# A graph attention layer: key/value rows made once and gathered, groups of 16 nodes split in two halves, scored and summed in four 32-row column tiles

## The chip, the cores and the metric

The kernel runs on one core of one Trainium2 chip. The metric is the device time of the whole program in microseconds (us), a median of several runs. A profile is one execution taken by the hardware profiler. TensorE (PE) multiplies matrices and transposes; VectorE (DVE), ScalarE (ACT) and GpSimd (POOL) work on elements; SyncE (SP) and POOL issue the DMAs here.

## The reference, cut to what matters

`x` is 6250 x 256; there are 206250 edges with 64 attributes each, sorted by destination, 33 to a node on average. Eight heads of 32 columns. The part that the change touches:

```python
x0 = layernorm(x)
q = (x0 @ Wq.T + bq); k = (x0 @ Wk.T + bk); v = (x0 @ Wv.T + bv)   # each (n, 8, 32)
e = (edge_attr @ We.T).reshape(-1, 8, 32)
alpha = sum(q[dst] * (k[src] + e), axis=-1) / sqrt(32)             # per edge and head
ex = exp(alpha - amax[dst])
out = segment_sum((v[src] + e) * ex / denom[dst])                  # per node and head
```

A gated skip, two layer norms, a feed-forward net of 1024 and a small mixture of experts follow; they are the third stage.

## The kernel before

All is fp32. N is padded to 6272 nodes, NB = 49 blocks of 128; a block has GB = 8 groups of GN = 16 nodes. Each group has one window of CH = 640 edges (T = 5 tiles of 128) from the place where its edges begin; edges of other nodes in the window are masked by a comparison of `dst` with the node number (`neq`, L530).

**Stage 1** (L122 to L297) normalizes x into `xn_rows` in HBM, makes `qT` (queries, transposed, kept in SBUF) and finds where each group's edges begin (`offs`). It goes in seven chunks of seven row tiles.

**Stage 2** (L302 to L792) is a loop over blocks and, written out in it, over the eight groups (turn j). Weights are folded into the queries and out of the values: for each group `G` = q times Wk (per head) is made on TensorE (`g_piece`, L680), so that scores are `G` times normalized rows, and values are summed as rows of x and edge attributes (`pZ`, 128 rows = 16 nodes x 8 heads, 321 columns) and projected with WvT only once a block (L783 to L791). In turn j:

- SyncE waits for `slot_free` (L444) and issues the loads for group j+2: `dst` broadcast (L403), `edge_attrT` (L405), `edge_attr` (L406), then the indices `srci` for group j+3 (L397). Once a block `starts` (L410) reads offsets into registers.
- POOL waits for the same count and for the indices, and issues five indirect DMAs (`gather`, L490), each of 128 rows of `xn_rows`, for group j+2.
- TensorE: `scores` of group j+1 (L694: six matmuls of 320 columns into `pS`); then five `pZ` matmuls of group j (L763), whose last frees the slot, with the transposes of the gathered rows of group j+2 (`ft`, L688) and the pieces of `G` between them; then `pt` (L703, five transposes of the weights of group j+1) and `zt` (L737, three transposes of group j's sums).
- DVE: `neq`, the maximum over `pS` (L536), the copies `pt_out` (L542) and `zt_out` (L586); once a block the merge into `U` (L606, L608), for which TensorE's next `zt` waits.
- ACT: copies of the transposed rows `FT` and of `G` (L622), `Exp` of the scores (`weights`, L636), `Zs` (L666).

There are four slots `F` and `F3`, so loads run two groups ahead. The order on each engine is the written one. The loop around all blocks (`long_loop`, L387) runs again only if some group has more edges than CH.

**Stage 3** (from L794) is node-wise and reads `U` and `xn_rows`.

Of the kernel before, what the change touches and what calls it, by code (L numbers as in the profile page):

```python
# [45 lines left out]
def build(nc, a, out):  # L46
# [16 lines left out]
    FW = 3 * P  # L63
    ONE = D + DE
    FP = -(-(ONE + 1) // 4) * 4
    K3 = DE + 1 + GN
    ZW = D + DE + 1
# [9 lines left out]
    BC = -(-(NG + 1) // P)  # L77

    xn_d = nc.dram_tensor("xn_rows", [NP, D], F32, kind="Internal").ap()
    bound_d = nc.dram_tensor("bounds", [BC * P], I32, kind="Internal").ap()  # L80
    x_d = a["x"].rearrange("(b p) d -> p b d", p=P)
    xn_v = xn_d.rearrange("(b p) d -> p b d", p=P)
    dst_rows = a["dst"].rearrange("(r c) -> r c", c=P)
# [3 lines left out]
    def sem(name):  # L87
        return top.enter_context(nc.semaphore(name))
# [12 lines left out]
    with top:  # L101
# [10 lines left out]
        offs = sbt(top, "offs", [1, NG + GB], I32)  # L112
# [3 lines left out]

        mid = ExitStack()
        with mid:
            qT = sbt(mid, "qT", [P, KD, NP + P])
            with ExitStack() as s1:  # L120
                x_all = sbt(s1, "x_all", [P, NB, D])
                xs = sbt(s1, "xs", [P, W7, D])  # L122
                xT = sbt(s1, "xT", [P, KD, W7 * P])
# [6 lines left out]
                WqT = sbt(s1, "WqT", [P, KD, D])  # L130
                bq = sbt(s1, "bq", [P, KD])
# [12 lines left out]
                lens = sbt(s1, "lens", [1, NG])  # L144
                mlen = sbt(s1, "mlen", [1, 1])
                tp = [pst(s1, f"tp{i}", [P, KD, P]) for i in range(2)]
                pq = [pst(s1, f"pq{i}", [P, 4 * P]) for i in range(2)]

                x_landed, w_landed, first_landed = sem("x_landed"), sem("w_landed"), sem("first_landed")
                rows_gathered, bounds_stored, bounds_landed = sem("rows_g"), sem("bounds_stored"), sem("bounds_landed")  # L150
                tiles_seen, xs_free = sem("tiles_seen"), sem("xs_free")
                U_cleared = sem("U_cleared")
                store_turns1 = sem("store_turns1")
                stats_done, rstd_done, xn_ready, xn_stored = sem("stats_done"), sem("rstd_done"), sem("xn_ready"), sem("xn_st")
                tp_filled, tp_emptied, q_filled, q_emptied = sem("tp_f"), sem("tp_e"), sem("q_f"), sem("q_e")
                bval_ready, rowi_ready, start_ready = sem("bval_r"), sem("rowi_r"), sem("start_r")
                q_steps = [(h0, min(4, W7 - h0)) for h0 in range(0, W7, 4)]
                Q7 = len(q_steps) * KD

                with nc.Block() as block:  # L160
# [112 lines left out]
                    def _(pe):  # L273
# [3 lines left out]
                        with pe.Fori(0, N7) as i:  # L277

                            pe.wait_ge(q_emptied, i * Q7 + 1)
                            for j in range(W7):  # L280
                                pe.wait_ge(xn_ready, i * W7 + j + 1)
                                if j >= 2:
                                    pe.wait_ge(tp_emptied, i * W7 + j - 1)
# [1037 lines left out]
```

## Time and profile before

| | us |
|---|---|
| median of 3 runs | 5581.74 |
| lowest, highest | 5575.02, 5582.84 |
| span of the profiled execution | 5584.0 |
| TensorE busy (share) | 5115.2 (92%) |
| ACT busy | 2257.3 (40%) |
| DVE busy | 1934.3 (35%) |
| POOL busy | 1895.7 (34%) |

Busy time is that of an engine's own instructions; DMA issues on SyncE do not count as busy, and each has a duration of its own in the time line (SPq). TensorE's entries are matmuls (PE) and weight loads (PEld); their ends are modelled, so distances between starts are the safer measure. Idle time of an engine names what ended it in square brackets. "PEclk" is the granted TensorE clock as a share of 2.4 GHz.

### The profile page before, as it was taken

The numbers are of one execution on the slowest core, as the hardware profiler recorded it, in microseconds if no ns is written. First come the engines' busy times: TensorE is split into PE (matmuls) and PEld (weight loads), VectorE is DVE, ScalarE is ACT, GpSimd is POOL, SyncE is SP. The second block draws the span as 40 slices with busy tenths as digits, with TensorE's granted clock in tenths as the row PEclk, the third lists the DMA queues.
The fourth block names the chain that finished last, engine by engine and source line by source line (L and its number), as shares of the span: only waits on it lengthen the run. The fifth ranks groups of instructions, "written<-read, shape, count | busy, mean of one in ns | idle before, by whom it ended". The sixth has DMA issues, their size and how long they took to land. (4 is left out here: it accounts for less than half of the span.)

```text
span 5584.0 us, 76757 instructions
## 1 busy us (share of the span) xinstructions
PE 5115.2 (92%) x22479; PEld 3611.0 (65%) x22479; DVE 1934.3 (35%) x4447; ACT 2257.3 (40%) x4140; POOL 1895.7 (34%) x2013
## 2 busy tenths in 40 slices
PE   4899999999999999999999999999999677877778
PEld 2577777777777777777777677777776454544545
DVE  3233233233333333333333332322333445445454
ACT  2344444444444444444444444444444323233233
POOL 1444444444444444444444444444443000000000
PEclk9899999999999999999999999999999877788778
DMA  2333333333333333333333433433433100000000
GB/s 102 94 103 96 96 100 98 97 98 94 102 96 96 103 95 95 102 92 95 103 95 95 105 94 92 104 93 96 103 94 86 61 13 20 13 13 20 13 13 7
DMA packets 486457, 445.39 MB, mean 80 GB/s; under 512 B 359613, under 2 KB 389310, under 8 KB 486408
## 3 DMA queue, kind: packets, MB, share of 16 engines
q0 software_dynamic: 96384, 265.00, 17.4%
q1 hardware_dynamic: 390024, 179.92, 12.8%
q14 instruction: 41, 0.34, 0.0%
q8 instruction: 8, 0.13, 0.0%
HBM read 431.89 MB, written 12.82 MB: 80 GB/s over the span
## 5 line engine op out<-in xcount | busy, mean ns | idle before, releaser
L494 POOL DMA_INDIRECT F<-xn_rows,srci x1970 | 1865.8, 947 | 2283.6 <-PE pZ L763 1799.4
L622 ACT ACTIVATE FT<-ring 128x256 f32<-128x256 f32 x1970 | 1196.9, 653 | 2328.9 <-PE ring L691 2327.2
L763 PE MATMUL pZ<-F,PT 128*128 128x321 f32 x3920 | 1380.7, 434 | 0.0
L699 PE MATMUL pS<-FT,G 128*128 128x320 f32 x3144 | 1096.0, 474 | 78.0 <-ACT FT L622 77.6
L699 PEld LDWEIGHTS pS<-FT,G 128*128 128x128 f32 x3144 | 613.0, 205 | 371.4 <-issue 202.2
L546 DVE COPY PT<-pPT 128x384 f32<-128x384 f32 (+1 forms) x786 | 348.8, 485 | 1327.8 <-PE pPT L706 1327.8
L691 PEld LDWEIGHTS ring<-ident,F 128*128 128x128 f32 x3940 | 481.5, 141 | 493.8 <-ACT FT L622 221.9
L691 PE MATMUL ring<-ident,F 128*128 128x128 f32 x3940 | 775.7, 282 | 7.4 <-DMA F<-xn_rows,srci 6.3
L763 PEld LDWEIGHTS pZ<-F,PT 128*128 128x128 f32 x3920 | 668.5, 191 | 105.0 <-issue 1.6
L539 DVE TENSOR_REDUCE nmx<-pS 128x1 f32<-128x640 f32 x393 | 324.0, 824 | 940.0 <-PE pS L699 935.3
L699 PE MATMUL pS<-F,G 81*128 81x320 f32 x1572 | 585.0, 454 | 0.0
L639 ACT ACTIVATE Pw<-pS,nMn 128x640 f32<-128x640 f32 x393 | 531.1, 1351 | 7.1 <-DVE nMn L540 7.1
L699 PEld LDWEIGHTS pS<-F,G 81*128 81x128 f32 x1572 | 319.4, 203 | 141.9 <-issue 28.2
L787 PE MATMUL pM<-WvT,ZT 128*128 128x33 f32 (+1 forms) x2352 | 365.7, 326 | 5.1
L787 PEld LDWEIGHTS pM<-WvT,ZT 128*128 128x128 f32 (+1 forms) x2352 | 359.1, 246 | 16.8 <-DVE ZT L589 16.8
L928 POOL DMA_DIRECT2D out_dram<-accb x6 | 5.8, 959 | 1072.5 <-DVEq L1093 1072.5
L706 PE MATMUL pPT<-ident,Pw 128*128 128x128 f32 x1965 | 279.4, 273 | 2.5 <-ACT Pw L639 2.5
L589 DVE COPY ZT<-pM 128x384 f32<-128x384 f32 x392 | 214.9, 548 | 192.2 <-PE pM L744 192.2
L622 ACT ACTIVATE G<-ring 128x256 f32<-128x256 f32 (+1 forms) x595 | 252.6, 425 | 13.4 <-PE ring L685 13.3
L685 PE MATMUL ring<-qh,Wk 128*128 128x256 f32 x794 | 237.9, 382 | 11.2 <-DVE qh L552 11.2
L1204 PE MATMUL hid<-rT,W1T 128*128 128x512 f32 (+1 forms) x448 | 204.1, 616 | 35.5 <-ACT h L1136 27.8
L533 DVE TENSOR_SCALAR F<-F,nid 17x640 f32<-17x640 int32 x394 | 214.6, 545 | 56.1 <-DVE U L608 44.0
(180 smaller groups left out, 3975.2 us busy)
## 6 DMA issues: line engine op xcount, KB each, us to landing
F<-in_edge_attrT SPq DMA_DIRECT2D x394, 160.0 KB
F<-in_edge_attr SPq DMA_DIRECT2D x394, 160.0 KB, 3.8
F<-xn_rows,srci POOLq DMA_INDIRECT x1970, 2.8
F<-in_dst SPq DMA_DIRECT2D x394, 42.5 KB
srci<-in_src SPq DMA_DIRECT2D x395, 2.5 KB, 3.3
x_all<-in_x SPq DMA_DIRECT2D x1, 6272.0 KB, 22.1
xn_rows<-xs SPq DMA_DIRECT2D x7, 896.0 KB, 3.9
xnb<-xn_rows SPq DMA_DIRECT2D x7, 896.0 KB, 4.8
```

The costliest lines, as they stand in the source:

```text
L494: pool.indirect_dma_start(out=F[s][:, t, 0:D], out_offset=None, in_=xn_d, in_offset=bass.IndirectOffsetOnAxis(ap=srci[j % GB][:, t:t + 1], ...
L539: ch.step(dve.tensor_reduce(nmx[:, j:j + 1], pS[:, :, 0:SH], AX.XY, ALU.max, negate=True))
L546: dve.tensor_copy(PT[:, t0:t1, :], pPT[q][:, 0:(t1 - t0) * P].rearrange("p (t r) -> p t r", r=P)).then_inc(pt_emptied, 1)
L589: dve.tensor_copy(ZT[:, :, :, j * GN:(j + 1) * GN], pM[:, 0:FW].rearrange("p (k h n) -> p k h n", k=3, n=GN)).then_inc(zt_emptied, 1)
L622: act.activation(dst, src, ACT.Copy).then_inc(ring_emptied, 1)
L639: act.activation(Pw[:, :, :].rearrange("p t (a e) -> p a e t", a=2), pS[:, :, 0:SH].rearrange("p a (e t) -> p a e t", t=T), ACT.Exp, bias= ...
L685: pe.matmul(ring[n % 2][0:rows, 0:HR * P // 2], w, qh[half][:, c, :, :].rearrange("p r n -> p (r n)"), start=True, stop=True).then_inc(rin ...
L691: m = pe.transpose(ring[n % 2][:, k * P:(k + 1) * P], F[j][:, t, k * P:(k + 1) * P], ident[:, :])
L699: m = pe.matmul(pS[:, q, 0:SH], G[0:(P if k < KD else K3), k, j, :], f, start=(k == 0), stop=(k == 2))
L706: m = pe.transpose(pPT[q][:, (t - t0) * P:(t - t0 + 1) * P], Pw[:, t, :], ident[:, :])
L763: z = pe.matmul(pZ[:, 0:ZW], PT[:, t, :], F[s][:, t, 0:ZW], start=(t == 0), stop=(t == T - 1))
L787: pe.matmul(pM[:, h * CW:(h + 1) * CW], ZT[0:rows, k, h, :], WvT[0:rows, k, h, :], start=(k == 0), stop=(k == 2))
```

## The change

Stage 1 additionally projects every row tile with [Wk, Wv] into `kv_rows` (512 columns: keys and values in blocks of 64, biases added by DVE) in HBM, and writes the scaled queries to `q_cols` in HBM instead of SBUF. x lands in seven pieces in `U`, whose clearing POOL does chunk by chunk; the masks are built here.

Stage 2 keeps 392 groups of 16 nodes, but a group consists of two halves of ON = 8 nodes with windows of OW = 320 edges each; `offs` has an entry for each half. The gather takes 512 columns of `kv_rows` in place of 256 of `xn_rows`, still five indirect DMAs of 128 rows. Scores: rows of `pS` are four strips of 32 (two sets of four heads x two halves), each written by its own matmul of 320 columns, twice (queries times keys; `G3` times edge attributes and mask). `pS` is 384 columns wide (320 + 64 of overlap of the halves). The sums `pZ` are 3 x 4 matmuls of 192 columns, each into 32 rows. `Pw` has three transposes, `Zs` two. The per-block projection becomes `project`, run in turn 0 of the next block, and the merge in its turn 1. SyncE loads each half by itself and fetches 64 queries twice a block.

```diff
+    ON = GN // 2
+    NO = 2 * NG
+    OW = CH // 2
+    HP = P // 2
+    SW = OW + HP
+    KB = SW // P
+    KV = 2 * D
+    FP = KV + DE
+    ZW = P + DE
...
+                            for j in range(W7):
+                                project_rows(i, j)
+                                if i + 1 < N7:
+                                    transpose_rows(i + 1, j)
...
-                            sp.dma_start(srci[j % GB][:, :], a["src"][bass.ds(o, CH)].rearrange("(p t) -> p t", t=T)
-                                         ).then_inc(idx_landed[j % GB], 16)
+                            s, done = srci[j % GB], idx_landed[j % GB]
+                            sp.dma_start(s[:, 0:TO], a["src"][bass.ds(oa, TO * P)].rearrange("(t p) -> p t", p=P)).then_inc(done, 16)
+                            sp.dma_start(s[0:HP, TO:TO + 1], src_t[bass.ds(oa, HP)].rearrange("(p t) -> p t", t=1)).then_inc(done, 16)
+                            sp.dma_start(s[HP:P, TO:TO + 1], a["src"][bass.ds(ob, HP)].rearrange("(p t) -> p t", t=1)).then_inc(done, 16)
+                            sp.dma_start(s[:, TO + 1:T], src_b[bass.ds(ob, TO * P)].rearrange("(t p) -> p t", p=P)).then_inc(done, 16)
...
+                            for o, at in enumerate((oa, ob)):
+                                cols = slice(o * OW, (o + 1) * OW)
+                                sp.dma_start(F3[s][DE:K3, cols].bitcast(I32), dst_t[bass.ds(at, OW)].partition_broadcast(GN)
+                                             ).then_inc(f3_landed[s], 16)
+                                sp.dma_start(F3[s][0:DE, cols], a["edge_attrT"][:, bass.ds(at, OW)]).then_inc(f3_landed[s], 16)
+                            sp.dma_start(F[s][:, 0:TO, KV:FP], a["edge_attr"][bass.ds(oa, TO * P), :].rearrange("(t p) d -> p t d", p=P)
                                          ).then_inc(ea_landed[s], 16)
+                            sp.dma_start(F[s][0:HP, TO, KV:FP], ea_t[bass.ds(oa, HP), :]).then_inc(ea_landed[s], 16)
+                            sp.dma_start(F[s][HP:P, TO, KV:FP], a["edge_attr"][bass.ds(ob, HP), :]).then_inc(ea_landed[s], 16)
+                            sp.dma_start(F[s][:, TO + 1:T, KV:FP], ea_b[bass.ds(ob, TO * P), :].rearrange("(t p) d -> p t d", p=P)
+                                         ).then_inc(ea_landed[s], 16)
...
                         def scores(j, s):
 
+                            half, g = j // HB, (j % HB) * 2
+                            for x in range(2):
+                                for c in range(KD):
+                                    for o in range(2):
+                                        r = c * HP + o * C
+                                        rows, cols = slice(r, r + C), slice(o * HP, o * HP + OW)
+                                        if x == 0:
+                                            m = pe.matmul(pS[rows, cols], qh[half][:, c, g + o, :],
+                                                          FT[j % 2][:, c, o * OW:(o + 1) * OW], start=True, stop=False)
+                                        else:
+                                            m = pe.matmul(pS[rows, cols], G3[half][0:K3, c, g + o, :],
+                                                          F3[s][0:K3, o * OW:(o + 1) * OW], start=False, stop=True)
                             m.then_inc(s_done, 1)
...
+                        def z_part(s, t):
+
+                            for c in range(KD):
+                                for o in range(2):
+                                    rows = slice(c * HP + o * C, c * HP + (o + 1) * C)
+                                    blocks = F[s][:, o * TO + t, :].rearrange("p (x d) -> p x d", d=BLK)
+                                    f = blocks[:, 2:9:3, :] if c == 0 else blocks[:, 6:9, :]
+                                    m = pe.matmul(pZ[rows, 0:ZW].rearrange("p (x d) -> p x d", d=BLK), PT[:, t, rows], f,
+                                                  start=(t == 0), stop=(t == KB - 1))
+                            return m
...
+                            for c in range(KD):
+                                pe.matmul(byhead[:, c * HR:(c + 1) * HR, 0:C], outT[:, c, :, :].rearrange("p a n -> p (a n)"),
+                                          ident[:, :].rearrange("p (h c) -> p h c", c=C), start=(c == 0), stop=False)
+                            for h in range(HR):
+                                pe.matmul(pairs[:, :, h, 0:C], zeaT[:, h, :, :].rearrange("p a n -> p (a n)"), WeP[:, h, :].rearrange("p (k c) -> p k c", k=KD),
+                                          start=False, stop=False)
...
                                     for t in range(KB):
                                         z = z_part(s, t)
                                         if t == KB - 1:
                                             z.then_inc(slot_free, 1)
                                         if t == 0:
                                             pe.wait_ge(gathered[s2], it * (16 * T * 2) + 16 * T * ((j + 2) // SLOTS + 1))
                                         pe.wait_ge(ring_emptied, rb + (m + t - 1))
                                         ft(s2, t, RING0 + m + t)
```

## Rows read from the trace of the kernel before

**Rows 1.** The page's part 1: busy us, share of the span, instructions.
```profile
PE 5115.2 (92%) x22479; PEld 3611.0 (65%) x22479; DVE 1934.3 (35%) x4447; ACT 2257.3 (40%) x4140; POOL 1895.7 (34%) x2013
```

**Rows 2.** Line 606, the merge: duration min/median/max ns, first and last start us.
```profile
L606 DVE TENSOR_TENSOR Utmp<-U,pM x49: 428/429/430, 268.1 to 4322.3; 128x264 f32<-128x264 f32 x49
```

**Rows 3.** Windows: stretch and its length, each engine's busy us, clock, DMA.
```profile
core 0: us, PE busy (x) PEld busy (x) DVE busy (x) ACT busy (x) POOL busy (x), PEclk, DMA share, GB/s
2000.00:2084.40 84.40, 82.73 (x393) 60.01 (x392) 26.00 (x58) 36.40 (x70) 37.88 (x40) 0.94 0.38 98
...
2039.30:2045.10 5.80, 5.80 (x13) 3.76 (x14) 1.40 (x3) 0.00 (x0) 0.00 (x0) 0.52 0.00 0
...
6.00:20.00 14.00, 0.00 (x0) 0.00 (x0) 7.66 (x10) 0.00 (x0) 4.03 (x4) 1.00 1.09 387
```

**Rows 4.** Time line of TensorE over one turn: start us, us, what, xcount.
```profile
2002.54 0.71 PE L706 MATMUL pPT<-ident,Pw 128*128 128x128 f32 x5
2003.09 0.49 PE L744 MATMUL pM<-ident,Zs 128*128 128x128 f32 x3
2003.80 1.31 PE L699 MATMUL pS<-FT,G 128*128 128x320 f32 x4 [0.23 <-ACT FT L622]
...
2007.12 0.70 PE L763 MATMUL pZ<-F,PT 128*128 128x321 f32 x2
2007.66 0.38 PE L691 MATMUL ring<-ident,F 128*128 128x128 f32 x2
...
2011.55 0.71 PE L706 MATMUL pPT<-ident,Pw 128*128 128x128 f32 x5
```

**Rows 5.** Time line of TensorE, the projection at a block's end.
```profile
2031.44 7.61 PE L787 MATMUL pM<-WvT,ZT 128*128 128x33 f32 x48
```

**Rows 6.** Waits of SyncE's queue: us in total, times, longest.
```profile
SPq L444 <- PE pZ L763: 3016.6, 390, 28.9
```

**Rows 7.** Time line of SyncE's queue: index load, then a group's loads.
```profile
147.88 0.47 SPq L397 DMA_DIRECT2D srci<-in_src  x1
148.47 0.26 SPq L403 DMA_DIRECT2D F<-in_dst  x1
148.83 0.49 SPq L405 DMA_DIRECT2D F<-in_edge_attrT  x1
149.51 0.59 SPq L406 DMA_DIRECT2D F<-in_edge_attr  x1
150.29 0.49 SPq L397 DMA_DIRECT2D srci<-in_src  x1
```

**Rows 8.** Line 411, reads of offsets into registers: duration min/median/max ns.
```profile
L411 SPq TENSOR_LOAD <-offs x50: 892/2052/2097, 144.3 to 4212.1; - x50
```

**Rows 9.** The page's part 6: DMA issues, KB each, us to landing.
```profile
F<-xn_rows,srci POOLq DMA_INDIRECT x1970, 2.8
...
srci<-in_src SPq DMA_DIRECT2D x395, 2.5 KB, 3.3
```

**Rows 10.** Time line of POOL: a gather of 512 B rows, two of 1 KB.
```profile
15.66 0.96 POOL L191 DMA_INDIRECT drow<-in_dst,rowi  x1 [0.30 <-issue]
...
2003.05 0.95 POOL L494 DMA_INDIRECT F<-xn_rows,srci  x1 [3.69 <-PE pZ L763]
...
2004.30 0.95 POOL L494 DMA_INDIRECT F<-xn_rows,srci  x1 [0.30 <-issue]
```

**Rows 11.** DMA queues from 2000 to 2084 us: packets, MB, share of engines.
```profile
q0 software_dynamic: 1886, 5.17, 22.8%
q1 hardware_dynamic: 7184, 2.99, 15.2%
```

**Rows 12.** Time line of TensorE in stage 1: projections of two chunks.
```profile
84.78 6.18 PE L294 MATMUL pq<-xT,WqT 128*128 128x512 f32 x16
...
94.98 6.18 PE L294 MATMUL pq<-xT,WqT 128*128 128x512 f32 x16
```

More of the change, by code:

```diff
@@ L233, in _ @@
[L233 to L245 removed]
+                        dve.wait_ge(bias_landed, 16 * (3 + KD))
@@ new lines, in project_rows @@
+                        def project_rows(i, j):
+                            n = i * W7 + j
+                            if n >= 3:
+                                pe.wait_ge(kv_emptied, n - 2)
+                            for f in range(KD):
+                                m = pe.matmul(pkv[n % 3][:, :], xT[i % 2][:, f, j * P:(j + 1) * P], Wkv[:, f, :],
+                                              start=(f == 0), stop=(f == KD - 1))
+                            m.then_inc(kv_filled, 1)
+                        for j in range(W7):
+                            transpose_rows(0, j)
@@ L410, in starts, with load_q @@
+                        def load_q(half, first):
+                            sp.dma_start(qb[half][:, :, :], q_v[:, :, bass.ds(first, HP)]).then_inc(qb_landed[half], 16)
                         def starts(first, n):
@@ L649, in _ @@
                         for j in range(2):
-                            for t in range(T):
-                                ft_out(j, t, n, n + 1)
+                            for q in range(len(PAIRS)):
+                                ft_out(j, q, n, n + 1)
                                 n += 1
                         weights(0, 1)
-                        with long_loop(act) as e0:
-                            ps = e0 // CH
+                        longest, loop = long_loop(act)
+                        with loop as e0:
+                            ps = e0 // OW
@@ L688, in ft, with g3 @@
-                        def ft(j, t, n):
-                            for k in range(KD):
-                                m = pe.transpose(ring[n % 2][:, k * P:(k + 1) * P], F[j][:, t, k * P:(k + 1) * P], ident[:, :])
+                        def g3(half):
+                            for c in range(KD):
+                                m = pe.matmul(pM[0:DE, c * HR * HP:(c + 1) * HR * HP], We[:, c, :],
+                                              qh[half][:, c, :, :].rearrange("p x r -> p (x r)"), start=True, stop=True)
+                            m.then_inc(g3_filled, 1)
```

759 lines of the change are left out of this document (423 added, 336 removed).

## The prediction

> **What bounds the kernel now.** I read the page's busy shares first: TensorE is busy 92% of the span, no other engine over 40% [rows 1]. A share over the span hides stages, so next the turns. The merge at L606 runs 49 times, the first at 268.1 us, the last at 4322.3 us [rows 2]: 4054.2 / 48 = 84.5 us for a block of 128 nodes, 10.56 us for one of its eight groups, and 49 x 84.47 = 4139 us for the middle stage. Ahead of it lie 268.1 - 84.5 = 184 us, behind it the remaining 1261 us; the change leaves the third stage alone, so all is decided in the middle. The windows say the same: one block of 84.4 us has TensorE 82.7 us busy and POOL 37.9, ACT 36.4, DVE 26.0 [rows 3].
>
> The time line of TensorE shows what a turn is made of [rows 4]. From one `pPT` burst (2002.54) to the next (2011.55) is 9.01 us. Six score matmuls of 320 columns take 2003.80 to 2007.12, 0.553 us each. A `pZ` matmul of 321 columns has its follower 0.54 us later (2007.12 to 7.66), so one of 256 columns counts 0.43; five transposes of `Pw` take 0.55 (2002.54 to 3.09), 0.11 each. Each fp32 matmul is two MATMUL records (x2), a transpose one. Eight turns of 9.01 make 72.1 us, but a block takes 84.5: the missing 12 us are the projection, 24 small matmuls in 7.6 us (0.32 us each) [rows 5], and the scores behind it, 5.8 us for what else takes 3.3, at a granted clock of 0.52, the 1.2 GHz level, where the block's mean is 0.94 [rows 3]. Before that fall TensorE had run short matmuls and weight loads.
>
> Last the queues, off the path today, since SyncE and POOL both wait for `pZ` [rows 6, 10]. A group's four loads are issued start to start 0.59 (indices, 147.88 to 148.47), 0.36 (dst), 0.68 (attrT) and 0.78 us (attr) [rows 7]: 2.4 us. Once a block SyncE reads nine offsets into registers: 2.05 us, and for three of them 0.89 [rows 8]. POOL issues five gathers, 1.25 us apart (2003.05 to 4.30): 6.25 us [rows 10].
>
> **The change, part by part.** *Does the new width fit?* The windows shrink from 640 to 320 edges for 8 nodes, and the loop repeats everything if one half has more. I counted dst of the reference's drawn inputs (seed 0): the longest run of an aligned eight nodes is 308. One pass, as before.
>
> *TensorE in a turn.* Columns after the change, if four 32-row column tiles truly run side by side: scores 2 x 0.553 = 1.11; `pZ` 3 x 192 columns, 3 x 0.54 x 192/321 = 0.97; ten transposes of keys 1.10; three of `Pw` 0.33; two of `Zs` 0.22; `g3` four matmuls of 256 columns a block, 4 x 0.43/8 = 0.21; `project` eight matmuls a block at the projection's 0.32, 0.32. Sum 4.26 us against 10.56. If the tiles run one after another: 8 x 0.553 + 12 x 0.323 + the same 2.18 = 10.48 us. The trace has no 32-row tile, so these are the two ends; the side-by-side end is no cheaper than the streamed columns. I take it, because the tiles of a group of four write different rows of PSUM and nothing in the program makes one wait for another; both ends stay in the range. At the lower clock of [rows 3] (5.8 us for 3.3) the 4.26 would become up to 8.5. The Trainium skill, "TensorEngine Tiling (Array Packing)", Key Properties, says that different tiles can load weights and multiply in parallel, but also that changing the tiling mode drains the engine; the first gives the 4.26, the second would add to it six times a turn, since full-array transposes stand between the tiled parts, and at rival C's price for a stop make it 5.2 to 5.9. No row here shows either.
>
> *SyncE.* This is what I expect to bind. Each load of a group is cut at the half boundary: dst 2, attrT 2, attr 4, indices 4, twelve DMAs for four. By the rows the time of an issue hangs little on size: 0.49 us for 64 rows of 2560 B, 0.59 for 640 pieces of 256 B, 0.47 to 0.49 for 128 rows of 20 B [rows 7]; only dst is at 0.26. So I take start to start 2 x 0.38 + 2 x 0.68 + 4 x 0.72 + 4 x 0.57 = 7.3 us, the attr halves a little under the whole. Low end, the short ones at attrT's 0.68 and the indices at 0.55: 7.0; high end, dst like attrT and all others like attr: 0.68 x 4 + 0.78 x 8 = 9.0. Added: two `load_q` a block, 2 x 0.75/8 = 0.19, and two register reads of ten values; from 0.89 for three and 2.05 for nine, 0.19 a value, so 2.25 each, 0.56 a turn. With a wait, 8.1 us (7.5 to 9.8). Queued behind each wait for `slot_free` are all twelve; who waits for them: DVE's `neq` (dst), TensorE's `pZ` (attr), and POOL, whose gather needs the indices that SyncE issues last. On the skill's page "DMA: Bandwidth & Descriptors", Rules for kernel authors, two transfers to disjoint partition halves are called not worth it, as both use the same 16 DMA engines; by it the halves gain nothing on the bus and cost their issue, which is the direction of this sum.
>
> *POOL.* Five gathers still, with rows of 2 KB for 1 KB. 128 rows of 512 B took 0.96 us and 128 of 1 KB 0.95 [rows 10], so I take 1.25 start to start, 6.25 and some 0.2 of waits: 6.5 us. Hidden while SyncE needs 8.1; its bound if SyncE is cheaper.
>
> *DMA engines.* In a block q0 is 22.8% and q1 15.2% of 84 us [rows 11]: 2.39 and 1.60 us a turn. The gathers double to 1.31 MB: 4.8 us at today's share for each byte, 3.4 at the 387 GB/s of the early `x_all` load [rows 3]. q1 has 7184/8 = 898 packets a turn now [rows 11] and about 1500 after (640 indices of 4 B one by one): 1.6 to 2.7 us. Together 5.0 to 7.5 us of a turn. At 8.1 they are 62 to 93% busy, so landings lengthen.
>
> *Does the chain fit?* Index DMA issued, lands 3.3 us later; five gathers 6.25; the last lands 2.8 us on, more under load [rows 9]; then transposes and `pZ` 1.5: about 14.5 us, within which SyncE has two more turns, 16.2. It fits with little slack. What makes SyncE's turn start is `slot_free`, three turns apart.
>
> *ACT and DVE.* They are 36.4/8 = 4.55 and 26.0/8 = 3.25 us busy a turn now [rows 3], and the change takes columns from both: `Exp`, the maximum and `PT` go from 640 columns to 384, the 1280 key columns go out in three copies for five, the `G` pieces and the `ZT` copies go; added are `halves_out`, six copies of at most 256 columns twice a block, and `g3_out`. So both stay under 4.6 us and hidden behind 8.1. Were the 8.1 gone, the chain scores, maximum, Exp, transposes would be next, at some 5 us.
>
> *Stage 1.* TensorE takes 10.2 us for seven row tiles now (84.78 to 94.98), 6.18 of it for 3584 projected columns, 1.72 ns a column [rows 12]. The key/value rows add 14 matmuls of 512 columns, 12.4 us: 7 x 20.1 = 141 us for 74. That is +67; with x landing in pieces and its statistics ahead of the bounds the loop should start some 24 us sooner (the two waits on DMA round trips leave its path), and the last store adds 6: +49 us (20 to 90; the added stores are 19 MB). DVE's and ACT's work of a chunk, each under half of TensorE's 20 us by [rows 3]'s shares, lies beside it. POOL's mask constants move here, beside that work. Prologue of the middle stage: gathers dominate as now, 0.
>
> *Sum*, against the profiled 5584 us: 5584 - 4139 + 392 x 8.1 + 49 = 4669 us. The runs' median 5581.74 is within 0.05% of the span, so I keep the number: 4670.
>
> **The rivals.** (A) *SyncE is cheaper than its rows, POOL or the DMA engines bind.* For: half-size loads have fewer descriptors, dst shows 0.26. Against: 20-byte rows cost as much as 2560-byte ones. 6.3 to 7.4 us a turn, at 6.9: 5584 - 4139 + 2705 + 49 = 4200. (B) *TensorE stays the bound*, because tiles overlap only in part or the clock falls to the level of [rows 3]. For: TensorE would be half idle, and its clock fell once already. Against: a turn at the low clock is 8.5, only just over SyncE. 9 to 10.2 us, at 9.6: 5260. (C) *Slower: tiles in series, and a stop at each change between tiled and full array.* Place: the six changes in a turn between scores or `pZ` and the transposes. Price: 10.48 plus six times 0.16 to 0.27 (two `pZ` records span 0.70 us where their follower starts after 0.54 [rows 4]; one half is 0.27), 11.4 to 12.1; at 11.7: 5584 - 4139 + 4586 + 49 = 6080. It decides from 10.44 us a turn on (4139 - 49 over 392). For: the columns in series are already 10.48. It is here that the drain of the skill's "TensorEngine Tiling (Array Packing)" page would act. Against: nothing in the program orders the tiles. (D) *A second pass*, if some half exceeded 320: twice the loop, near 7800. The count speaks against it.
>
> **How the numbers follow.** Forecast (SyncE, 7.5 to 8.8 us: 4430 to 4940) 0.50; A (4000 to 4430) 0.22; B (5000 to 5500) 0.18; C 0.08; D and others slower 0.02. Slower than before 0.09, within 0.2% (about what a measurement of this kernel can tell from no change) 0.01, faster 0.90. The predicted time is the likeliest case's 4670; the range leaves out C, D, the top of B and the lowest part of A: 4100 to 5350.
>
> **What would show it.** Right: the L606 successor spaced about 65 us a block; SyncE's DMA starts without gaps over 1 us; TensorE idle before the transposes on a gather or before `pZ`, busy share under 70%; four MATMUL records of a `pZ` quartet starting within 0.4 us. A: POOL gathers without gaps at 1.25 us. B: TensorE over 90% busy with PEclk low. C: quartets spaced as the sum of four. Wrong altogether: SyncE's short DMAs at 0.3 us, or gathers of 2 KB rows longer than 0.95 us to issue.

## The result, and the profile after

The changed kernel takes 5456.15 us (median of 4 runs, 5444.12 to 5460.82) against 5580.15 of the kernel before in the same measurement: ratio 0.9773, 95% interval 0.9759 to 0.9787. It is 2.3% faster, 786 us above the forecast of 4670 and 106 us above the top of the stated range, 5350. The page of its profiled execution, beside [rows 1] and [rows 11]:

```profile
span 5459.2 us, 88133 instructions
...
PE 4078.0 (75%) x26117; PEld 2169.5 (40%) x26117; DVE 1766.1 (32%) x4373; ACT 1362.9 (25%) x3251; POOL 1925.3 (35%) x2075
...
PEclk9777777777777777777777777777777887788778
DMA  5566666666666666666666666666665000000000
...
q0 software_dynamic: 159520, 523.41, 32.3%
q1 hardware_dynamic: 715732, 205.36, 17.7%
```

TensorE lost a fifth of its busy time, from 92% of the span to 75%, and nothing else became full. The merge is at L689 now; its instructions, beside [rows 2] (durations in ns, then first and last start in us):

```profile
L689 DVE TENSOR_TENSOR Utmp<-U,pM x50: 428/429/431, 239.6 to 4198.2; 128x264 f32<-128x264 f32 x50
```

The 49 spacings take 3958.6 us, 80.8 us each, 10.10 us a turn. The first merge of the new order stands in turn 1 of block 0 (it has nothing to add yet) and the last behind the loop, so the 49 spacings hold 391 turns and not 392: a turn is really 10.12. Turns below are all spacings divided by eight; for the changed kernel and what is made from it they are thus some 0.3% low, which no comparison rests on.

Because the merge moved, the stages are better parted at the first and last `pZ` matmul (before, then after):

```profile
L763 PE MATMUL pZ<-F,PT x3920: 431/433/436, 188.8 to 4312.3; 128*128 128x321 f32 x196
```

```profile
L850 PE MATMUL pZ<-F,PT x9408: 322/350/530, 224.0 to 4189.4; 128*32 128x192 f32 x196
```

What lies ahead of the first grew by 35 us, the middle stage fell from 4123.5 to 3965.4 us, by 158, and what lies behind it changed by 2 (1271.7 and 1269.8 us).

The waits say who is late: first those of the compute engines, then SyncE's own for `slot_free`, which were 3016.6 us before [rows 6] (total us, times, longest):

```profile
ACT FT L758 <- remote: 2059.4, 286, 9.6
POOL F L604 <- DMA srci<-in_src: 1467.2, 349, 46.2
...
DVE nmx L656 <- remote: 561.1, 148, 5.6
...
PEld pZ L850 <- issue: 452.7, 1457, 1.5
```

```profile
SPq L587 <- PE pZ L850: 144.0, 86, 4.7
...
SPq L587 <- remote: 86.5, 108, 1.7
```

SyncE hardly waits any longer: it is the queue that binds, and POOL waits for the indices that SyncE issues last. But one kind is new, "remote" on ScalarE and VectorE, and TensorE's weight loads for `pZ` wait 452.7 us for nothing that the profile shows. SyncE's time line shows the same from the other side, beside [rows 7]:

```profile
2005.10 0.44 SPq L545 DMA_DIRECT2D F<-in_edge_attr  x1
2006.17 0.69 SPq L547 DMA_DIRECT2D F<-in_edge_attr  x1
2008.34 0.01 SPq L548 DMA_DIRECT2D F<-in_edge_attr  x1
2009.77 0.00 SPq L549 DMA_DIRECT2D F<-in_edge_attr  x1
2010.48 0.68 SPq L532 DMA_DIRECT2D srci<-in_src  x1
2011.21 0.49 SPq L533 DMA_DIRECT2D srci<-in_src  x1
2011.87 0.47 SPq L534 DMA_DIRECT2D srci<-in_src  x1
```

From 2011.21 on an issue follows the last one after 0.66 us; between 2005.10 and 2010.48 four steps take 5.4 us. I call this a slow stretch. In one, every instruction of SyncE, also one that moves no data, takes some 0.7 us or a multiple, and the streams of other engines crawl too: in this one TensorE's `pZ` records start 0.7 us apart, one by one (2009.82, 2010.52), and ScalarE's copy at 2011.38 has 7.26 us of "remote" before it. POOL is the exception: its gathers go on at 1.25 us start to start (2003.89 to 2008.89). The clearest mark is the register MOVE in front of each DMA (min/median/max in ns). Kernel before, then after:

```profile
L406 SPq MOVE F<-in_edge_attr x394: 29/29/37, 147.0 to 4295.3; - x197
```

```profile
L548 SPq MOVE F<-in_edge_attr x394: 2/29/866, 206.0 to 4176.7; - x197
```

This stretch begins 2.3 us after POOL starts a round of five gathers (2003.89) and ends 2.3 us after the last is issued (2008.89). Nearly every turn has one; others begin up to 6 us into the round and are shorter.

The tiles themselves did what was hoped. TensorE's time line, beside [rows 4]; the first three lines at the granted clock 0.50, the last three at 1.00:

```profile
2028.89 1.30 PE L831 MATMUL pS<-FT,qh 128*32 128x320 f32 x8
2029.96 1.29 PE L834 MATMUL pS<-F,G 80*32 80x320 f32 x8
2031.03 0.87 PE L850 MATMUL pZ<-F,PT 128*32 128x192 f32 x8
...
2036.30 0.75 PE L831 MATMUL pS<-FT,qh 128*32 128x320 f32 x8
2036.87 0.72 PE L834 MATMUL pS<-F,G 80*32 80x320 f32 x8
2037.41 0.51 PE L850 MATMUL pZ<-F,PT 128*32 128x192 f32 x8
```

Four matmuls of 320 columns (x8: two records each) take 0.57 and 0.54 us (2036.30 to 2036.87 to 2037.41), the time of one before the change.

### The profile page after: what moved, and what is told of

It reads as the page before. It is cut to its first block and busy times, and to the rows that moved or that the text cites. A ratio compares the mean times of both kernels' runs of the same rounds, so it can differ in the third digit from the quotient of the medians.

```text
span 5459.2 us, 88133 instructions
## 1 busy us (share of the span) xinstructions
PE 4078.0 (75%) x26117; PEld 2169.5 (40%) x26117; DVE 1766.1 (32%) x4373; ACT 1362.9 (25%) x3251; POOL 1925.3 (35%) x2075
## 5 line engine op out<-in xcount | busy, mean ns | idle before, releaser
L604 POOL DMA_INDIRECT F<-kv_rows,srci x1970 | 1880.9, 955 | 2147.4 <-DMA srci<-in_src 1467.2
L758 ACT ACTIVATE FT<-ring 128x512 f32<-128x512 f32 (+1 forms) x1182 | 581.8, 527 | 2990.7 <-remote 2059.4
L850 PE MATMUL pZ<-F,PT 128*32 128x192 f32 x9408 | 810.0, 390 | 93.5 <-issue 92.0
L662 DVE COPY PT<-pPT 128x384 f32<-128x384 f32 x393 | 219.0, 557 | 1600.1 <-PE pPT L840 1197.3
L656 DVE TENSOR_REDUCE nmx<-pS 128x1 f32<-128x384 f32 x393 | 219.0, 557 | 1027.8 <-remote 561.1
L850 PEld LDWEIGHTS pZ<-F,PT 128*32 128x32 f32 x9408 | 284.7, 125 | 493.8 <-issue 452.7
L831 PE MATMUL pS<-FT,qh 128*32 128x320 f32 x3144 | 436.6, 641 | 14.2 <-issue 12.1
L834 PE MATMUL pS<-F,G 80*32 80x320 f32 x3144 | 415.7, 612 | 0.0
L650 DVE TENSOR_SCALAR F<-F,nid 16x640 f32<-16x640 int32 x394 | 223.0, 566 | 58.3 <-issue 31.8
L764 ACT ACTIVATE Pw<-pS,nMn 128x384 f32<-128x384 f32 x393 | 226.3, 576 | 9.1 <-DVE nMn L657 4.3
```

Of the source, the lines that this page charges most:

```text
L604: pool.indirect_dma_start(out=F[s][:, t, 0:KV], out_offset=None, in_=kv_d, in_offset=bass.IndirectOffsetOnAxis(ap=srci[j % GB][:, t:t + 1] ...
L650: dve.tensor_scalar(F3[j][DE:K3, :], F3[j][DE:K3, :].bitcast(I32), nid[DE:K3, c], None, ALU.not_equal).then_inc(neq_done, 1)
L656: ch.step(dve.tensor_reduce(nmx[:, j:j + 1], pS[:, 0:SW], AX.X, ALU.max, negate=True))
L758: act.activation(FT[j % 2][:, :, t0 * P:t1 * P], ring[n % 2][:, 0:KD * w].rearrange("p (k e) -> p k e", e=w), ACT.Copy).then_inc(ring_empt ...
L764: act.activation(Pw[:, :], pS[:, 0:SW], ACT.Exp, bias=nMn[:, j:j + 1], accum_out=lsum[:, j:j + 1]).then_inc(p_done, 1)
L831: m = pe.matmul(pS[rows, cols], qh[half][:, c, g + o, :], FT[j % 2][:, c, o * OW:(o + 1) * OW], start=True, stop=False)
```

## The experiments

The kernels were measured in five batches; the kernels of a batch ran one after another on one chip, with the kernel before beside them (5606.65, 5582.11, 5583.03, 5577.74 and 5599.76 us in batches 1 to 5). Batches 2 and 3 had the same chip. Some edits gather or load other edges than the layer needs, to time a part by itself; where that is so it is said. Times are medians; a turn is the spacing of the merges divided by eight.

**Batch 1: what are the slow stretches made of?**

*Gathered bytes halved.* 1 KB rows of `xn_rows` are gathered; the value columns are zeros.

```diff
-                                    out=F[s][:, t, 0:KV], out_offset=None, in_=kv_d,
+                                    out=F[s][:, t, 0:D], out_offset=None, in_=xn_d,
```

> The gather takes 256 columns of xn_rows again in place of 512 of kv_rows (1 KB rows for 2 KB; the value columns stay zero, so the sums are not the reference's); all else is the changed kernel. Theory T: SyncE's queue sets the turn, 12 issues of about 0.65 us, and a stretch of 2 to 3 us in each turn in which all engines' instructions come only every 0.7 us, which comes with the DMA engines at a share near 1, so with the gathered bytes. T expects no such stretch, a turn of 8.0 to 8.5 us for 10.12, and 4650 to 4850 us in all. Rival R1, the stretches come from the many 4-byte and short descriptors of SyncE: still over 5300. Rival R2, TensorE and its low clock bind: 5400 to 5460.

5478.65 us, ratio 0.9768 (0.9724 to 0.9813), turn 10.16, "remote" ahead of ScalarE's copy still 1943.6 us, while the DMA engines' share fell from 0.64 to 0.42. The expected 4650 to 4850 us did not come: the gathered bytes are not the cause.

*Order.* Indices issued ahead of the edge loads.

```diff
-                                    load_edges(at[k], at[k + 1], j + 2)
                                     load_indices(at[k + 2], at[k + 3], j + 3)
+                                    load_edges(at[k], at[k + 1], j + 2)
```

> SyncE issues the four index loads of group j+3 ahead of the eight edge loads of group j+2; nothing else changes. T (throughput of SyncE's queue): the same twelve issues, so within 1% of 5456. Rival R3, the way of one group through slot, index load, gather and transposes is too long: the gather can start some 5 us sooner, so the turn falls by 1 us or more, to under 5100 us.

5457.25 us, turn 10.07: no change, so R3 falls. POOL's wait for the indices is a mark of SyncE's rate, not a chain of its own.

*One index DMA for four* (other edges for part of the second half).

```diff
-                            sp.dma_start(s[:, 0:TO], a["src"][bass.ds(oa, TO * P)].rearrange("(t p) -> p t", p=P)).then_inc(done, 16)
...
+                            sp.dma_start(s[:, :], a["src"][bass.ds(oa, CH)].rearrange("(p t) -> p t", t=T)).then_inc(done, 16)
```

> The indices of a group come in one DMA of 128 rows of 20 B from the first half's start, as before the change, in place of four with 640 pieces of 4 B (so other rows are gathered than the reference needs; the same number of bytes). T: SyncE issues nine DMAs for twelve, 1.9 us less; the stretches stay; a turn of 8.2 to 8.7 us, 4700 to 4900 us in all. R1 (short descriptors make the stretches): these go as well, 6.5 to 7.2 us, 4150 to 4400. R2: 5400 to 5460.

5157.36 us, turn 9.33. Three issues fewer are worth 0.77 us a turn, less than half of their 1.9 us, where 4700 to 4900 us had been expected. The stretches stay, so R1, the 4-byte descriptors, falls.

*Plain loads for the gathers.* The same bytes into the same tiles, 128 neighbouring rows each instead of the gathered ones.

```diff
-                                pool.indirect_dma_start(
-                                    out=F[s][:, t, 0:KV], out_offset=None, in_=kv_d,
-                                    in_offset=bass.IndirectOffsetOnAxis(ap=srci[j % GB][:, t:t + 1], axis=0),
-                                ).then_inc(gathered[s], 16)
+                                r0 = (j * T + t) % (NB - 1) * P
+                                pool.dma_start(F[s][:, t, 0:KV], kv_d[r0:r0 + P, :]).then_inc(gathered[s], 16)
```

> POOL's five indirect DMAs become five plain DMAs of 128 neighbouring rows of 2 KB of kv_rows, the same bytes into the same places (other rows than the reference needs). T, bytes make the stretches: they stay, 5300 to 5500 us. Rival R4, the indirect descriptors or scattered rows make them: they go, a turn of 8.0 to 8.5 us, 4650 to 4850 us.

4652.24 us, ratio 0.8295 (0.8269 to 0.8321). The merge, SyncE's MOVE, and SyncE's time line of one group:

```profile
L687 DVE TENSOR_TENSOR Utmp<-U,pM x50: 428/429/431, 230.1 to 3387.1; 128x264 f32<-128x264 f32 x50
```

```profile
L545 SPq MOVE F<-in_edge_attr x394: 29/29/29, 202.5 to 3366.5; - x197
```

```profile
2004.28 0.38 SPq L532 DMA_DIRECT2D srci<-in_src  x1
...
2006.88 0.33 SPq L542 DMA_DIRECT2D F<-in_dst  x1
...
2009.16 0.46 SPq L545 DMA_DIRECT2D F<-in_edge_attr  x1
...
2011.74 0.38 SPq L532 DMA_DIRECT2D srci<-in_src  x1
```

No slow stretch; twelve issues in 7.46 us without a gap, 8.05 us a turn, at more DMA traffic than the changed kernel has (212 against 168 GB/s from 1500 to 2500 us). So R4 holds: without the indirect gathers there are no stretches, and SyncE binds at the predicted 8.1. The edit changes three things at once, and no run parts them: the addressing by indices, the scattered rows, and POOL's pace (0.53 us start to start for 1.25).

**Batch 2: is it the number of SyncE's loads?** Q says yes, G says the gathers alone.

*Four loads.* SyncE's twelve back to four of the form before (other edges for the second half).

```diff
+                            sp.dma_start(F3[s][DE:K3, :].bitcast(I32), dst_t[bass.ds(oa, CH)].partition_broadcast(GN)
+                                         ).then_inc(f3_landed[s], 16)
+                            sp.dma_start(F3[s][0:DE, :], a["edge_attrT"][:, bass.ds(oa, CH)]).then_inc(f3_landed[s], 16)
...
```

> Edit: the changed kernel with SyncE's twelve loads of a group put back to four of the form that the kernel before had (one index load, one dst, one attrT, one attr, 640 neighbouring edges); the five indirect gathers of 2 KB rows stay. It reads other edges than the reference for the second half. Theory Q (many short SyncE issues beside the indirect gathers make the slow stretches, in which every engine's instructions come only every 0.7 us): SyncE's register move never lasts over 40 ns, the turn is GpSimd's or TensorE's, 6.5 to 7.2 us, and the run takes 4050 to 4350 us. Theory G (the indirect gathers of the changed kernel alone make them, however few the loads are): moves of up to 700 ns and more stay, ScalarE and VectorE still show idle time ended by 'remote', and the turn is 8 to 8.7 us, 4650 to 4900 us.

4166.60 us (ratio 0.7462, 0.744 to 0.7484), turn 6.82, MOVE at most 40 ns.

*The kernel before with twelve loads* (edge rows and edge scores come from different edges in part).

```diff
-                            sp.dma_start(srci[j % GB][:, :], a["src"][bass.ds(o, CH)].rearrange("(p t) -> p t", t=T)
+                            sp.dma_start(srci[j % GB][:, 0:2], a["src"][bass.ds(o, 256)].rearrange("(t p) -> p t", p=P)).then_inc(idx_landed[j % GB], 16)
...
```

> Edit: the kernel before, with the four SyncE loads of each group cut into twelve DMAs that bring the same data (index load in four, dst and attrT in two each, attr in four). All else is the kernel before. Twelve issues and the register reads come to 7.5 to 8.1 us, below that kernel's turn of 10.56 us. Theory Q (many short SyncE issues beside indirect gathers make the slow stretches): SyncE's register move, 29 to 37 ns in the kernel before, lasts up to 0.5 us and more, ScalarE and VectorE show waits ended by 'remote', and the run is slower than 5580 us by more than 1%, 5650 to 6200. Theory G (it takes what else the changed kernel has: 1 KB more for each gathered row, a faster turn): no move over 40 ns and 5570 to 5610 us.

5582.0 us, ratio 1.0 (0.9989 to 1.0011), MOVE at most 42 ns.

*Indices on ScalarE*, five groups ahead; the whole computation is kept.

```diff
-                                    load_indices(at[k + 2], at[k + 3], j + 3)
...
                                     act.activation(Zs[:, :], pZ[:, 0:ZW], ACT.Copy).then_inc(z_out, 1)
+                                    if j % 4 == 0:
+                                        aat = starts_on(mybir.EngineType.Activation, b * (2 * GB) + 2 * (j + 5), 8)
+                                    load_indices(act, aat[2 * (j % 4)], aat[2 * (j % 4) + 1], j + 5)
```

> Edit: the four index loads of a group are issued by ScalarE, two groups earlier, instead of by SyncE; SyncE issues eight. If SyncE's count of issues at 0.6 us (and 0.7 us and more in slow stretches) sets the turn: SyncE's share falls by a third, ScalarE has 2.6 us of issues more on 3.5 us busy, the turn falls from 10.1 to 8 us or less, 4600 to 4900 us. If the slow stretches set the turn and are a fixed 3 us beside whichever engine issues the DMAs: turn 9.2 to 10, 5100 to 5400 us. If ScalarE's own instructions, moved back by the issues, come late for TensorE: 5400 to 5700 us.

4265.24 us, ratio 0.7639 (0.7617 to 0.7661), turn 7.06, no stretch: more than any theory gave.

*Two of five gathers indirect*, the others plain loads of neighbouring rows.

```diff
+                                if t % 2:
                                     pool.indirect_dma_start(
...
+                                else:
+                                    r0 = (j * T + t) % (NB - 1) * P
+                                    pool.dma_start(F[s][:, t, 0:KV], kv_d[r0:r0 + P, :]).then_inc(gathered[s], 16)
```

> Edit: of the five gathers of a group two stay indirect (tiles 1 and 3), three are plain DMAs of 128 neighbouring rows of the same size (these read other rows than the reference). Five indirect gave 5456 us, none 4652. If each indirect gather adds its share: 5456 - 3/5 x 804 = 4974, 4900 to 5050 us, with moves of SyncE of 0.5 us and more, but for a shorter part of the turn. If the slow stretch needs a backlog of several indirect gathers: 4650 to 4750 us and no move over 40 ns. If one or two are enough to start a full one: 5200 us or more.

4736.31 us, ratio 0.8482 (0.8458 to 0.8507), turn 8.28, one MOVE of 98 ns, all others under 40.

These four do not agree: the first came out as Q had said, the kernel before with twelve loads as G had said (5570 to 5610 us; Q had 5650 or more). They were read as facts about the kernels even so, and S and L below were made to fit them. That was false, as batch 4 shows: in this batch nothing had slow stretches.

**Batch 3: which of SyncE's loads?** S: SyncE's queue being full brings the stretches. L: indices that land just ahead of the gathers do.

*All twelve on SyncE, indices five groups ahead.*

```diff
-                                        at = starts(b * (2 * GB) + 2 * (j + 2), 2 * (HB + 1))
+                                        at = starts(b * (2 * GB) + 2 * (j + 2), 2 * HB + 6)
...
+                                    load_indices(sp, at[k + 6], at[k + 7], j + 5)
```

> Edit: SyncE still issues all twelve DMAs of a group, but the four index loads five groups ahead instead of three, so that GpSimd never waits for a fresh index. Four kernels without slow stretches (four loads: 4167 us; indices on ScalarE five groups ahead: 4265; two of five gathers indirect: 4736; no indirect: 4652) leave two readings. Theory L (the lead: the slow stretches come when GpSimd's gathers are let go one by one by indices that have just landed, so that gathers and SyncE's issues run in step): no register move over 40 ns, SyncE back to back at 8.1 us a turn, 4650 to 4750 us. Theory S (SyncE's queue filled to the last with twelve issues a turn beside indirect gathers, whatever is ordered first): slow stretches as before, moves of up to 700 ns and more, turn 9.8 to 10.3, 5350 to 5480 us.

5471.98 us, turn 10.10, MOVE up to 1406 ns. L falls.

*The attr loads on ScalarE, indices left on SyncE.*

```diff
+                                    if j % 4 == 0:
+                                        aat = starts_on(mybir.EngineType.Activation, b * (2 * GB) + 2 * (j + 3), 8)
+                                    load_attr(act, aat[2 * (j % 4)], aat[2 * (j % 4) + 1], j + 3)
```

> Edit: the four attr loads of a group are issued by ScalarE, one group earlier; SyncE keeps the two dst, two attrT and the four index loads, three groups ahead. The order of index load and gather stays as in the changed kernel. Theory S (SyncE's queue filled to the last): SyncE has eight issues, 5.3 us, no slow stretches, turn near 7.0, 4200 to 4350 us, like the indices on ScalarE (4265). Theory L (fresh indices just ahead of the gathers): slow stretches stay, register moves over 0.5 us, 4700 us or more.

5182.17 us, turn 9.37, MOVE up to 1524 ns. SyncE has the eight issues of the 4265 us kernel and stretches all the same: S falls as well.

*Indices on ScalarE, but three groups ahead.*

```diff
-                                        aat = starts_on(mybir.EngineType.Activation, b * (2 * GB) + 2 * (j + 5), 8)
-                                    load_indices(act, aat[2 * (j % 4)], aat[2 * (j % 4) + 1], j + 5)
+                                        aat = starts_on(mybir.EngineType.Activation, b * (2 * GB) + 2 * (j + 3), 8)
+                                    load_indices(act, aat[2 * (j % 4)], aat[2 * (j % 4) + 1], j + 3)
```

> Edit: as the kernel whose index loads ScalarE issues five groups ahead (4265 us), but three groups ahead, as SyncE did. Theory S (SyncE's queue filled to the last): no slow stretches, since SyncE has eight issues, and at most GpSimd's wait for the index, 4250 to 4500 us. Theory L (fresh indices): register moves over 0.5 us and 4700 us or more.

8851.84 us, ratio 1.5858: neither theory gave such a time. Its waits:

```profile
POOL F L611 <- DMA srci<-in_src: 5073.9, 393, 46.1
...
PE ring L828 <- DMA F<-kv_rows,srci: 4255.0, 394, 14.9
```

ScalarE issues the indices of group j+3 behind the `Zs` copy of group j, which stands behind the key copies of group j+2; the key copies of j+3, one turn on, need the gather that needs those indices. Index issues, landing, five gathers and their landing then fit into one turn, one after another: 18.75 us. Two groups more of lead take them off that path.

This kernel also has next to no stretches, in a batch that has them: "remote" ahead of ScalarE's copy comes once, 1.9 us, and from 300 us on SyncE's MOVE keeps to 38 ns:

```profile
L551 SPq MOVE F<-in_edge_attrT x772: 29/38/38, 308.9 to 7541.2; - x193
```

Its five gathers a turn are the same. But in the turn at 2000 us SyncE's eight issues end at 2003.38 and start again at 2016.98, while the gathers run from 2004.16 to 2009.15. At its start, where SyncE's loads do lie beside the gathers, it has a stretch (up to 211.09 us). Whether it is the slow pace or the lack of overlap that keeps the stretches away, no run tells.

Comparing the start of these kernels gave the next step. With the indices on ScalarE in either form, SyncE issues the same DMAs in the same order up to 208 us, and POOL's first gathers start at 197.49 and 196.79 us; yet only the one of batch 3 has a stretch there.

**Batch 4: batch or build?**

*The changed kernel and the one with the indices on ScalarE again, side by side.*

> No edit: the changed kernel again, beside the other kernels of this batch. Theory B (batch: where or when a program is loaded decides whether the slow stretches come, whatever its code): it comes out either near 5456 us with register moves of 0.7 us, as in its first measurement, or at 4200 to 4700 us without them, and the other three kernels of this batch go the same way. Theory K (kernel: its own code or order of DMAs decides): 5440 to 5470 us again, while the kernel with the indices on ScalarE stays at 4265.

> No edit against the kernel in which ScalarE issues the four index loads five groups ahead (4265 us, no slow stretches). Theory B: if the changed kernel beside it has slow stretches, this one has them too, SyncE's register moves last up to 0.7 us and more, and it takes over 4600 us, some 5000. Theory K: 4250 to 4280 us and no move over 40 ns.

The changed kernel: 5455.95 us again. The other, the same code that took 4265.24 us in batch 2: 5132.02 us (5 runs, 5091.91 to 5160.42), ratio 0.9201 (0.9179 to 0.9224), turn 9.31. Its start in batch 2 and in batch 4:

```profile
202.59 0.44 SPq L552 DMA_DIRECT2D F<-in_edge_attr  x1
203.22 0.49 SPq L554 DMA_DIRECT2D F<-in_edge_attr  x1
203.90 0.47 SPq L555 DMA_DIRECT2D F<-in_edge_attr  x1
204.55 0.45 SPq L556 DMA_DIRECT2D F<-in_edge_attr  x1
205.09 0.41 SPq L549 DMA_DIRECT2D F<-in_dst  x1
205.60 0.47 SPq L551 DMA_DIRECT2D F<-in_edge_attrT  x1
```

```profile
202.93 0.44 SPq L552 DMA_DIRECT2D F<-in_edge_attr  x1
203.55 0.49 SPq L554 DMA_DIRECT2D F<-in_edge_attr  x1
205.03 0.45 SPq L555 DMA_DIRECT2D F<-in_edge_attr  x1
206.45 0.01 SPq L556 DMA_DIRECT2D F<-in_edge_attr  x1
206.48 0.70 SPq L549 DMA_DIRECT2D F<-in_dst  x1
208.59 0.01 SPq L551 DMA_DIRECT2D F<-in_edge_attrT  x1
```

The same instructions, 0.65 us apart in one batch and up to 2.1 us in the other. And its MOVE over the run, batch 2, then batch 4:

```profile
L552 SPq MOVE F<-in_edge_attr x394: 29/29/38, 202.5 to 2979.7; - x197
```

```profile
L552 SPq MOVE F<-in_edge_attr x394: 3/29/880, 202.9 to 3870.9; - x197
```

*Rows moved, code longer.* Against the layout of data and code as the cause; the gathered rows lie up to 333 KB further on.

```diff
-    xn_d = nc.dram_tensor("xn_rows", [NP, D], F32, kind="Internal").ap()
+    xn_d = nc.dram_tensor("xn_rows", [NP + 333, D], F32, kind="Internal").ap()[0:NP, :]
```

```diff
+                            for _ in range(64):
+                                sp.sem_inc(load_turns, 1)
```

> Edit: the changed kernel with its tensor xn_rows 333 rows longer, so that the gathered kv_rows behind it may lie 333 KB further on. Theory B: as the changed kernel of this batch, within 0.5%. If where the gathered rows lie against the code makes the slow stretches: no register move over 40 ns and 4600 to 4700 us where the changed kernel has 5456, or some other time in between.

> Edit: the changed kernel with 64 semaphore increments behind SyncE's loop, which run once (some 2 to 3 us); they make SyncE's code longer and move what lies behind it. Theory B: as the changed kernel of this batch, plus up to 5 us. If where the code lies makes the slow stretches: 4600 to 4700 us without them.

5455.81 and 5451.23 us: neither matters. Nor is code being loaded in the stretches by the queues that the page calls "instruction" (q8, q14): from 310 to 4200 us the changed kernel's DMA traffic is q0 and q1 alone. Whether a kernel that is open to the stretches has them is thus a condition of the batch, and the comparisons between batch 2 and batches 1 and 3 had compared batches. It is not the chip alone: batches 2 and 3 had the same one.

**Batch 5: what makes a kernel open to the condition?** The kernel before is not: its times differ by 0.5% between the five batches.

> No edit: the changed kernel again, as the mark of this batch. If the batch has the slow stretches (four of five batches so far had them): 5440 to 5470 us, SyncE's register moves up to 0.7 us and more. If it has none: SyncE's twelve issues set the turn at 8.1 us, as in the kernel with plain loads (4652 us), and it takes 4640 to 4720 us, the 4670 of the prediction within 1%.

> No edit against the kernel with SyncE's loads in four DMAs (4167 us in the batch without slow stretches). In a batch with them: if SyncE's many issues cause them, no register move over 40 ns and 4160 to 4180 us again. If the five indirect gathers at this pace suffice: moves of 0.5 us and more, turn 8 to 9 us, 4650 to 5050 us. In a batch without them: 4160 to 4180 us.

> No edit against the kernel before with its loads cut into twelve DMAs (5582 us in the batch without slow stretches). In a batch with them: if twelve SyncE issues beside five indirect gathers of any size cause them, moves of 0.5 us and more and 5600 us or more, since its turn has 2.5 us of slack for SyncE but TensorE stands still too. If it takes the changed kernel's pace or bytes: no move over 50 ns, and 5570 to 5610 us.

This batch had the stretches. The changed kernel took 5490.92 us (ratio 0.9807, 0.9778 to 0.9835); four loads 4882.19 (0.8719, 0.8679 to 0.876; batch 2: 4166.60), turn 8.62, with 1291.6 us of "remote" ahead of ScalarE's copy; the kernel before with twelve loads 6026.95 (1.0764, 1.0733 to 1.0795; batch 2: 5582.0), turn 11.66 against 10.55. The last one's MOVE here, beside at most 38 ns for the same line in batch 2:

```profile
L410 SPq MOVE F<-in_edge_attr x394: 5/29/719, 150.7 to 4730.9; - x197
```

So under the condition twelve loads beside five gathers of 1 KB rows, at the old pace, are enough to slow the kernel before by 8%, where its own four loads cost it nothing; and four loads are no protection either once the turn is near 7 us. What the stretches cost, where one kernel was seen with and without: 2.25 us a turn (indices on ScalarE), 1.80 (four loads), 1.11 (the kernel before with twelve).

## Why the prediction was wrong

- **The step that failed** is the assumption under all of SyncE's sum, that an issue costs what it costs in [rows 7] however many stand beside the gathers. The sum itself holds: 8.05 us a turn with plain loads, 8.28 with two indirect gathers and the same twelve loads, against 8.1. The changed kernel has 10.10. The 2.05 us between, times 392, are 804 us; in batch 1 the changed kernel with only the order of its loads altered and the one with plain loads differ by 5457 - 4652 = 805, and the forecast missed by 786. The missing term is the slow stretch, and no row of before shows one.
- **How much of the miss belongs to the batch is not shown.** The changed kernel was measured three times over, never in a batch without stretches. An estimate from the kernel with two indirect gathers in batch 2, whose SyncE issues are the same: 5456 - 392 x (10.10 - 8.28) = 4743 us. Whether it would take that was not tried.
- **SyncE binds:** right. Its waits for `slot_free` fell from 3016.6 to some 230 us, and with stretches present its issues still count: twelve give a turn of 10.10 us, nine and eight 9.31 to 9.37, four 8.62. With four it no longer binds: it waits 2118 us for `slot_free`, and the turn is long because the other engines crawl.
- **TensorE's 4.26 us:** the tiles' overlap is right (0.57 and 0.54 for 0.553), so the low end was the right end to take, but the sum was short of the stops. The four-load kernel of batch 2 shows a turn at full clock:

```profile
2006.75 0.53 PE L841 MATMUL pZ<-F,PT 128*32 128x192 f32 x8
2007.21 0.65 PE L809 MATMUL ring<-ident,F 128*128 128x128 f32 x4
2007.80 0.53 PE L841 MATMUL pZ<-F,PT 128*32 128x192 f32 x8
2008.26 0.44 PE L809 MATMUL ring<-ident,F 128*128 128x128 f32 x2
```

192 columns take 0.46 us where columns alone give 0.32, and four transposes 0.59 for 0.44: some 0.14 us at each change between tiled and full array, and none from tiles to tiles (0.54 for scores followed by `pZ`, as before). Six make 0.84, and 4.26 + 0.84 = 5.10; the turn from 2002.51 to 2009.81, less 2.05 us of waiting for a gather, is 5.25. The Trainium skill, "TensorEngine Tiling (Array Packing)", Key Properties, says that changing the mode drains the engine and that different tiles run in parallel: this trace agrees with both. The low end of the 5.2 to 5.9 that the prediction worked out by that page, at rival C's price, was the better number; at 8.1 us of SyncE it would have changed nothing.
- **Rival C** (series): false. **Rival B** (TensorE bound, 5260): its time is nearer than mine, its reason is not; TensorE is 75% busy, and its granted clock, 0.77 from 1500 to 2500 us, is 0.89 there with plain loads, where it has the same matmuls. **Rival D:** false, one pass. **Rival A** (6.9 us, 4200) is what comes once SyncE has fewer issues and the batch no stretches: 7.06 and 6.82 us, 4265 and 4167, of which POOL's five gathers take 6.25, at a DMA share of 0.85.
- **POOL:** 2 KB rows still issue in 0.95 us, 1.25 start to start: right. **DMA engines:** 0.64 of a turn of 10.1 is 6.5 us, within 5.0 to 7.5. The Trainium skill's "DMA: Bandwidth & Descriptors", Rules for kernel authors, calls two transfers to disjoint partition halves not worth it; here only the two pieces of 64 rows in the index and attr loads are such halves, the other cuts go by columns or tiles. The issue time that all the cuts cost is seen (twelve in 7.46 us for four in 2.4), and no run shows a gain beside it: in batch 5 four loads take 4882 us where twelve take 5491.
- **Stage 1:** the first score matmul starts 43.5 us later (172.8 to 216.3), for +49: right in size. The prologue behind it, taken as unchanged, is 8 us shorter, which leaves the +35 up to the first `pZ`. All in all 5584 + 35 - 158 - 2 = 5459.

## A version that beats both

The four index loads on ScalarE, five groups ahead: 5132 us beside the changed kernel's 5456 in batch 4 (0.9201 of the kernel before), and 4265 in batch 2 (0.7639).

## What to carry to other kernels

Cutting loads in pieces turns bytes into issues: count every issue of the queue at its start-to-start time, and give part of them to an engine with idle time, early enough that no turn has to contain their whole latency (two groups of lead less took this kernel from 4265 to 8852 us). And when two kernels differ in a way that the code doesn't explain, run the same code again beside them before building a theory: two theories here, S and L, rested on a difference between batches, and the kernel before, which ran in each, gave no sign of it.

## What the runs showed of the hardware

- In some batches the instruction streams of SyncE and TensorE slow to about one instruction in 0.7 us, for up to some 5 us at a time, while indirect gathers are issued and moved, and ScalarE and VectorE stand idle with "remote" as what ends the wait; POOL's gathers keep their 1.25 us. It was so in four of five batches here, and not with plain DMAs of the same bytes (MOVE at most 38 ns). Half of the bytes, another order, data moved by up to 333 KB or longer code don't alter it. The kernel before, with four loads in a turn of 10.6 us, and a kernel with gathers and SyncE's loads one after another in a turn of 18.75 us don't show it. What the condition is (where a program is placed, what else goes on on the chip) stays open, and so does what the gathers share with the instruction streams.
- Four 32-row column tiles of fp32 run fully side by side, and a change between tiles and full array costs some 0.14 us at a granted clock of 1.00.
